# Attention and non-local block in fp32r pairs: score tiles over three bank pairs, the sum row at the batch's head, the second half's residual rows kept whole

## What is computed

```python
q = x1.T @ Wq.T + bq                     # 1024 x 64
k = Wk @ x2 + bk                         # 64 x 1024
v = Wv @ x2 + bv                         # 512 x 1024
xm = v @ softmax(q @ k, axis=1).T + x1   # 512 x 1024
g, theta, phi = convs of x2, xm, x2      # 256 x 1024 each, with their biases
y = (theta.T @ phi / 1024) @ g.T         # no softmax here
out = gamma * (Ww @ y.T + wb - mean) / sqrt(var + 1e-5) + beta + xm
```

## Time and profile before

| | us |
|---|---|
| median of 3 runs | 1065.98 (1063.28 to 1066.46) |
| profiled execution | 1065.61 |
| its span | 1063.8 |
| TensorE busy | 1042.0 (98%) |
| VectorE, ScalarE, GpSimd busy | 722.1, 480.6, 280.5 |

### The profile page before, as it was taken

The page is one execution under the profiler, slowest core; times in us unless marked ns, Lnnn a source line. Parts: engine busy times, 40 slices in busy tenths (PEclk is TensorE's granted clock), DMA queues, the critical chain, the costliest instruction groups (busy, mean ns, idle before and its releaser), DMA issues.

```text
span 1063.8 us, 13869 instructions
## 1 busy us (share of the span) xinstructions
PE 1042.0 (98%) x5104; PEld 850.5 (80%) x5104; DVE 722.1 (68%) x961; ACT 480.6 (45%) x810; POOL 280.5 (26%) x199
## 2 busy tenths in 40 slices
PE   6999999999999999999999999999999999999997
PEld 4688887888778887788877888778887888878886
DVE  6885388844888448884488745886368863788625
ACT  7753355434444345533545325453265532555411
POOL 1412261123501235012360123502244022440220
PEclk9999999999999999999999999999999999999999
DMA  6535251360513605236152351423424344243502
GB/s 237 169 78 143 107 198 43 75 217 27 195 42 73 215 29 197 50 89 198 41 178 58 106 175 64 155 72 106 160 70 149 80 112 146 81 140 78 136 23 79
DMA packets 80627, 122.06 MB, mean 115 GB/s; under 512 B 13104, under 2 KB 46384, under 8 KB 80560
## 3 DMA queue, kind: packets, MB, share of 16 engines
q1 hardware_dynamic: 80560, 121.17, 37.1%
HBM read 70.79 MB, written 16.78 MB: 82 GB/s over the span
## 4 chain that ended last, share of the span: by engine, by line
PE 88%; DVE 6%; DMA 3%; ACT 1%; issue 1%; SPq 0%; DVEq 0%; ACTq 0%
PE pG L573 33%; PE pG L472 13%; PE pG L584 8%; PE pG L480 6%; PE pG L513 4%; PE pG L487 4%; PE pT L594 3%; PE pS L525 3%; PE pT L525 2%; PE pG L594 2%; PE pM L552 2%; PE pM L561 2%; PE pS L451 2%; PE pT L462 2%; DVE xr L902 2%; DMA out_dram<-xr 1%
## 5 line engine op out<-in xcount | busy, mean ns | idle before, releaser
L573 PE MATMUL pG<-pt,vT 128*128 128x512 f32 x1536 | 352.9, 389 | 1.0 <-DVE pt L852 1.0
L573 PEld LDWEIGHTS pG<-pt,vT 128*128 128x128 f32 x1536 | 287.2, 188 | 60.2 <-issue 1.2
L472 PE MATMUL pG<-wv,x2s 128*128 128x512 f32 x768 | 182.9, 393 | 0.5 <-DVE vT L799 0.4
L881 DVE SCALAR_TENSOR_TENSOR xr<-pG,cl,xr 128x512 f32<-128x512 f32 x64 | 48.0, 751 | 189.2 <-PE pG L573 179.9
L931 POOL TENSOR_TENSOR xms<-xr,xms 128x512 fp32r<-128x512 f32 x64 | 87.7, 1370 | 319.6 <-ACT xms L726 319.6
L472 PEld LDWEIGHTS pG<-wv,x2s 128*128 128x128 f32 x768 | 142.1, 188 | 33.3 <-issue 3.3
L726 ACT ACTIVATE xms<-xr 128x512 fp32r<-128x512 f32 x64 | 40.3, 629 | 203.9 <-DVE xr L881 203.9
L852 DVE TENSOR_TENSOR pt<-mv,pt 128x512 fp32r<-128x512 f32 x128 | 89.8, 753 | 35.6 <-ACT pt L703 35.6
L923 POOL TENSOR_TENSOR x2Ts<-x2T_f,x2Ts 128x512 fp32r<-128x512 f32 x64 | 90.5, 1452 | 72.8 <-ACT x2Ts L672 72.7
L927 POOL TENSOR_TENSOR ys<-yf,ys 128x256 fp32r<-128x256 f32 x32 | 27.3, 854 | 306.1 <-ACT ys L694 306.1
L584 PE MATMUL pG<-xms,wth 128*128 128x512 f32 x384 | 90.1, 391 | 0.0
(11 more groups left out here) (112 smaller groups left out, 1420.9 us busy)
## 6 DMA issues: line engine op xcount, KB each, us to landing
mv<-tp SPq DMA_DIRECT2D x512, 64.0 KB, 2.0
...
```

Of the source, the lines that this page charges most:

```text
L472: last = mm(bank, x2s[:, l, c, 128 * m:128 * m + 128], wv[:, r, c, :], start=(c == 0 and n == 0), stop=(c == 3 and n == 2))
L573: last = mm(bank, vT[:, l, m, 128 * c:128 * c + 128], pt(h)[:, r, m, :], start=(m == 0 and n == 0), stop=(m == 7 and n == 2))
```

## The change

It has these parts:

1. Score tiles rotate over three bank pairs: pS, pT, pM. S:t waits for the exp of t-3 from t = 3 on. As pM has other uses, S:2 waits for the copy of gt, S:5 for the low part of GT:1, GT:0 for the exp of tile 2, and M for the exp of tile 5. The lists now have S:0 S:1 S:2, then S:3 S:4, then S:5 S:6 S:7 in batches 1 to 7, where they had S:0 S:1, S:2, S:3, S:4, S:5, S:6 S:7 with other work between.
2. gs stands after v:0 instead of before k, gt before S:0. Its row is kept in a buffer of its own (`grow_b`), which shares memory with the first half's output, so its copy waits for a store.
3. For the second half xr[c] is no longer given up after its split. A new ScalarE step xc:c adds the constant to it in place, wy:1,c multiplies by the gain and adds xr[c], and that is the output: there is no out:1,c. The first half is evicted into the place of the LO part of its own xms (`oh`), with semaphores s_so of its own for the stores; wy:1,c no longer waits for a store. k and q of the next batch wait for these stores. x2T:m waits for theta's last product instead of out:1,m//2.
4. All lists are reordered. In LATER ScalarE has x2T:0 ahead of k, and xs:3 after x1:3; VectorE makes the low part of the next batch's x2:3 between wy:1,1 and wy:1,2 (it was before wy:0,0), and s after k. In FIRST ScalarE has w:0 (rounding of wk) after x2:0, x2:1 and xs:0, and v:4 stands before S:0.

```diff
@@ FIRST (batch 0)
-        "k:0 k:1 v:0 v:1 q:0 q:1 v:2 v:3 S:0 S:1 v:4 S:2 L:0 L:1 L:2 S:3 L:3 gs S:4 G:0 G:1 gt G:2 G:3 v:5 S:5 "
-        "v:6 GT:0 S:6 GT:1 v:7 Y:0 S:7 Y:1 Y:2 Y:3 PV:0,0,0 M:0 PV:0,0,1 M:1 PV:0,1,0 PV:0,1,1 B:0 PV:0,2,0 B:1 "
+        "k:0 k:1 v:0 v:1 q:0 q:1 v:2 v:3 v:4 S:0 S:1 gs gt L:0 L:1 S:2 S:3 L:2 L:3 G:0 G:1 GT:0 S:4 G:2 G:3 v:5 "
+        "GT:1 v:6 S:5 v:7 Y:0 S:6 S:7 Y:1 Y:2 Y:3 PV:0,0,0 PV:0,0,1 PV:0,1,0 M:0 M:1 PV:0,1,1 PV:0,2,0 B:0 B:1 "
...
@@ LATER (batches 1 to 7), pe
-        "gs k:0 k:1 q:0 q:1 v:0 v:1 v:2 S:0 S:1 gt L:0 L:1 S:2 L:2 S:3 L:3 G:0 S:4 G:1 GT:0 G:2 G:3 v:3 S:5 v:4 "
-        "v:5 v:6 GT:1 v:7 Y:0 S:6 S:7 Y:1 Y:2 Y:3 PV:0,0,0 M:0 M:1 PV:0,0,1 PV:0,1,0 PV:0,1,1 B:0 B:1 PV:0,2,0 "
+        "k:0 k:1 q:0 q:1 v:0 gs v:1 v:2 gt S:0 S:1 S:2 L:0 L:1 L:2 L:3 S:3 S:4 G:0 G:1 GT:0 G:2 G:3 v:3 GT:1 v:4 "
+        "v:5 v:6 v:7 S:5 S:6 S:7 Y:0 Y:1 Y:2 Y:3 PV:0,0,0 PV:0,0,1 M:0 M:1 PV:0,1,0 PV:0,1,1 B:0 B:1 PV:0,2,0 "
...
@@ LATER, act
-        "xs:2 xs:3 s x1:2 x1:3 k x2T:0 x2T:1 x2T:2 q x2T:3 x2T:4 x2T:5 v:0 x2T:6 q2 v:1 k2 x2T:7 gs v:2 gt S:0 "
+        "xs:1 xs:2 x1:1 x2:3 x1:2 x1:3 xs:3 s x2T:0 k x2T:1 x2T:2 q x2T:3 x2T:4 v:0 gs q2 k2 x2T:5 v:1 gt x2T:6 "
+        "v:2 x2T:7 S:0 L:0 L:1 L:2 S:1 L:3 S:2 G:0 S:3 G:1 G:2 v:3 T:0 GT:0 v:4 T:1 v:5 GT:1 S:4 G:3 v:6 v:7 T:2 "
...
@@ LATER, dve
+        "k s q v:0 q2 k2 v:1 S:0 v:2 n:0 S:1 tr:0 S:2 n:1 tr:1 G:0 S:3 G:1 n:2 G:2 tr:2 G:3 S:4 n:3 v:3 tr:3 T:0 "
...
+        "th:0,0 B:1 th:0,1 +x2:0 th:1,0 +x2:1 +x2:2 th:1,1 wy:0,0 wy:0,1 out:0 out:1 wy:0,2 wy:0,3 out:2 out:3 "
+        "wy:1,0 wy:1,1 +x2:3 wy:1,2 wy:1,3"
...
+        oh = [at(f"oh{c}", [128, 512], F, rd + 4096 * c + 2048) for c in range(4)]
+        grow_b = at("grow_b", [128, 256], F, rd + 6144)
...
         def s_bank(t):
-            return pT if t % 2 else pS
+            return (pS, pT, pM)[t % 3]
...
             def do_GT(b, r):
                 if r == 0:
-                    wait(eng, "s_colc", b)
+                    wait(eng, "exp", b, 2)
...
             def do_S(b, t):
-                elif t >= 2:
-                    wait(eng, "exp", b, t - 2)
+                elif t == 2:
+                    wait(eng, "s_colc", b)
+                elif t >= 3:
+                    wait(eng, "exp", b, t - 3)
+                    if t == 5:
+                        wait(eng, "GTlo", b, 1)
...
             def do_M(b, k):
+                wait(eng, "exp", b, 5)
...
             def do_x2T(b, m):
                 if b:
-                    wait(eng, "oa", b - 1, 4 + m // 2)
+                    wait(eng, "g", b - 1, G_TH + 3)
...
+            def do_xc(b, c):
+                wait(eng, "xlo", b, 4 + c)
+                done(act(xr[c][:, :], xr[c][:, :], ACT.Identity, bias=cst(c)), "xc")
...
             def do_wy(b, h, c):
-                if h == 0:
-                    wait(eng, "xlo", b, 4 + c)
+                if h:
+                    wait(eng, "xc", b, c)
+                    done(stt(out=xr[c][:, :], in0=bank_of(i), scalar=gain(c), in1=xr[c][:, :],
+                             op0=ALU.mult, op1=ALU.add), "gf")
                 else:
-                    eng.wait_ge(s_st[c], 16 * (2 * b + 1))
-                done(stt(out=xr[c][:, :], in0=bank_of(i), scalar=gain(c), in1=xms(h)[:, c, LO, :].bitcast(F),
-                         op0=ALU.mult, op1=ALU.add), "gf")
+                    done(stt(out=oh[c][:, :], in0=bank_of(i), scalar=gain(c), in1=xms0[:, c, LO, :].bitcast(F),
+                             op0=ALU.mult, op1=ALU.add), "gf")
```

More of the change, by code:

```diff
@@ L236, in xattn_kernel @@
         s_st = [sem(f"s_st{i}") for i in range(4)]
+        s_so = [sem(f"s_so{i}") for i in range(4)]
         s_mv = [sem(f"s_mv{i}") for i in range(8)]
@@ L299, in pt_half @@
                     for t in range(2)]
-        grow = gram_f[2][0:2, 0:256]
+        grow = grow_b[0:2, :]
         def gram_turned(r):
@@ L421, in _ @@
                     for c in range(4):
-                        wait(eng, "oa", b, 4 * h + c)
-                        eng.dma_start(out[b, 128 * c:128 * c + 128, 512 * h:512 * h + 512], xr[c][:, :])\
-                           .then_inc(s_st[c], 16)
+                        dst = out[b, 128 * c:128 * c + 128, 512 * h:512 * h + 512]
+                        if h:
+                            wait_free(eng, b, G_WY + 4 + c)
+                            eng.dma_start(dst, xr[c][:, :]).then_inc(s_st[c], 16)
+                        else:
+                            wait(eng, "oa", b, c)
+                            eng.dma_start(dst, oh[c][:, :]).then_inc(s_so[c], 16)
             for c in range(4):
-                eng.wait_ge(s_st[c], 32 * NB)
+                eng.wait_ge(s_so[c], 16 * NB)
+                eng.wait_ge(s_st[c], 16 * NB)
         @block.tensor
@@ L628, in do_k @@
                 if b:
-                    wait(eng, "oa", b - 1, 3)
+                    for c in (0, 1):
+                        eng.wait_ge(s_so[c], 16 * b)
                 done(act(k1[0:64, :], pS[64:128, :, :], ACT.Copy), "t1k")
@@ L634, in do_q @@
                 if b:
-                    wait(eng, "oa", b - 1, 3)
+                    for c in (2, 3):
+                        eng.wait_ge(s_so[c], 16 * b)
                 done(act(q1[0:64, :], pT[64:128, :, :], ACT.Copy), "t1q")
@@ L706, in do_gs @@
             def do_gs(b):
-                wait(eng, "qlo", b)
                 wait(eng, "s_row", b)
+                if b:
+                    eng.wait_ge(s_so[1], 16 * b)
                 done(act(grow, pM[0:2, 1, 256:512], ACT.Copy), "s_rowc")
@@ L722, in do_B @@
                 done(act(bm[:, HI, k, :], pM[:, k, :], ACT.Copy), "Bhi")
+            def do_xc(b, c):
+                wait(eng, "xlo", b, 4 + c)
+                if b == 0:
+                    eng.wait_ge(s_cst, 4)
+                done(act(xr[c][:, :], xr[c][:, :], ACT.Identity, bias=cst(c)), "xc")
             def do_PV(b, h, c):
@@ L735, in _ @@
             do = dict(w=do_w, x2=do_x2, xs=do_xs, x1=do_x1, k=do_k, q=do_q, k2=do_k2, q2=do_q2, v=do_v, S=do_S, L=do_L, G=do_G,
-                      GT=do_GT, Y=do_Y, x2T=do_x2T, s=do_s, T=do_T, gs=do_gs, gt=do_gt, mts=do_mts, B=do_B, PV=do_PV,
+                      GT=do_GT, Y=do_Y, x2T=do_x2T, s=do_s, T=do_T, gs=do_gs, gt=do_gt, mts=do_mts, B=do_B, xc=do_xc, PV=do_PV,
                       th=do_th)
@@ L892, in do_wy, with do_out @@
                 wait(eng, "g", b, i)
-                if h == 0:
-                    wait(eng, "xlo", b, 4 + c)
-                else:
-                    eng.wait_ge(s_st[c], 16 * (2 * b + 1))
-                done(stt(out=xr[c][:, :], in0=bank_of(i), scalar=gain(c), in1=xms(h)[:, c, LO, :].bitcast(F),
-                         op0=ALU.mult, op1=ALU.add), "gf")
-            def do_out(b, h, c):
-                wait_free(eng, b, G_WY + 4 * h + c)
-                done(stt(out=xr[c][:, :], in0=xr[c][:, :], scalar=cst(c), in1=xms(h)[:, c, HI, :].bitcast(F),
+                if h:
+                    wait(eng, "xc", b, c)
+                    done(stt(out=xr[c][:, :], in0=bank_of(i), scalar=gain(c), in1=xr[c][:, :],
+                             op0=ALU.mult, op1=ALU.add), "gf")
+                else:
+                    done(stt(out=oh[c][:, :], in0=bank_of(i), scalar=gain(c), in1=xms0[:, c, LO, :].bitcast(F),
+                             op0=ALU.mult, op1=ALU.add), "gf")
+            def do_out(b, c):
+                wait_free(eng, b, G_WY + c)
+                done(stt(out=oh[c][:, :], in0=oh[c][:, :], scalar=cst(c), in1=xms0[:, c, HI, :].bitcast(F),
                          op0=ALU.add, op1=ALU.add), "oa")
```

8 lines of the change are left out of this document (4 added, 4 removed), and 38 rows, old and new, of tables (act, dve, pe).

## The result

The changed kernel takes 1079.76 us (median, 1075.69 to 1080.29), the kernel before 1065.94 in the same comparison: ratio 1.0126 [1.0097, 1.0156]. It is slower by 13.8 us, where the forecast was 6.9 faster. The span of its profiled execution is 1077.7 us, 13.9 more than before, so the profile carries the whole loss.

A forecast was written before the change was run, and what follows sets the result against it. TensorE, busy 98% of the span, was taken to bound the kernel. Switches -8.9, old heads -6.5, end -2.0, batch 0 +0.6 and new heads +9.9 gave -6.9 us, from 1065.61 to 1058.7; range 1050 to 1067.

The forecast's parts named there:

- Switching: Score tiles: grouping them saves 0.42 us per joined tile, 9.7 us, less 0.8 for lone sum-row transposes: -8.9 us.
- The end: End of the run: the last wy eviction is itself the output and ends near 1059.3: -2.0 us.
- The heads: Heads of later batches: 6.5 us of old losses in batches 2 to 4 go, new head waits add 9.9 us.
- +9.9 for the new heads: Heads of batches 1 to 7: q's copy late, 1.2 us each (8.4), plus 0.5 in each of three early batches (1.5).
- The upper bound: Later heads: at most 2.7 us lost each, x2T load issued at 24.9 and landing in 6.2 us; total 1067.7.
- The second rival: Later heads: GpSimd holds VectorE's x2:3 for one whole 2.4 us instruction, delaying k and q; slower, 1073.3 at 3.5 us; chance 0.15.
- The middle: Score tiles to PV: new waits of S:2, S:5, M and GT:0 ride behind long work, costed at nothing.
- th: Theta stage at the batch heads: the forecast gave it no gain or loss, taking 11.1 us as its length.
- Batch 0: First batch: later k and v +1.7, v:4 ahead of S:0 -1.7, transposes waiting for the sum row's copy +0.6; net +0.6 us.
- The first rival: Later heads run free, x2T:0 landing in time, so the 9.9 us fall away: 1048.8 us; chance 0.30.

The follow-up runs named there:

- rot_alone: Kernel before with only the three-pair rotation and the middle's new order; heads, output and ends kept as before: 1079.52 us, ratio 1.0140.
- pool_memset: Changed kernel with GpSimd filling x1's low part with zeros instead of subtracting, in batches 1 to 7: 1059.31 us, ratio 0.9953.
- before_memset: Kernel before with GpSimd's subtraction for x1's low part replaced by a zero fill in every batch but the first: 1060.85 us, ratio 0.9958.
- xr_first: Changed kernel with SP's four loads of x1's first half put ahead of the third group of 16 block moves: 1075.51 us, ratio 1.0104.
- all_fix: Changed kernel with x2:3, xs:3, k early, two x2T quarters before stores, xr loads earlier, PV:0,1 and tr:7 earlier on VectorE, batch 0 mended: 1092.34 us.
- wk_first: Changed kernel with w:0, the rounding of wk, first on ScalarE and VectorE in batch 0: 1080.31 us, ratio 1.0126.
- best3: best2 with th's first evictions moved ahead of the x2 splits, and on ScalarE ahead of xc:3: 1049.15 us, ratio 0.9849.
- best2: Changed kernel with the head laid out as before, k ahead of x2T:0, middle and batch 0 mended, x2T loads re-placed on SP: 1059.39 us, ratio 0.9931.
- x2_early: Changed kernel with x2:3's low part moved back ahead of wy and xs:3 right after xs:2: 1073.71 us, ratio 1.0069.

## Why the prediction was wrong, point by point

**Switching, -8.9: right.** From S:0 to the first PV the seven batches take 8.2 us less. Take out gt, which came in ahead of S:0 (its 1.5 us left this stretch), the 1.5 us by which batch 2 was slow before, and Y's new waits, which put PV 2.7 us later in five of them: -8.0, or 1.14 us a batch for the 1.15 forecast (seven times 0.1 for the transposes is 0.7, where I put 0.8). The gain is real, also in rot_alone.

**The end, -2.0: right** (-2.1).

**The heads, forecast +3.4 net (-6.5 and +9.9), measured +11.2.** That is the k and q rows of the table (20.7) less gs (6.5) and gt (1.5) that moved in, and less the 1.5 us of batch 2. Free stages would be 3.63 + 13.07; by that the new heads lose 18.9 us, 2.7 each, for the 1.4 that I put on them. Two steps failed, both in the term "+9.9 for the new heads". I let x2:3 be done "between 21.8 and 23.7" and used it only to time the x2T load; but TensorE begins k at 22.0 and needs that very part in its last matmuls. It was ready 25.3 us after th began in batch 3 (418.9 less 393.57), 1.6 beyond my bound, and 24.9 in four others, so k itself lost 2 us in five of seven batches. The rest of the chain was late with it: in batch 5 the load was issued 26.1 us after th began, was there at 30.4, and q's copy came at 33.6, for the forecast 24.2, 29.0 and 31.6. And I counted half an instruction of GpSimd in the way, where two output additions alone took 3.0 us more than free. Second, I checked S:0 and v:2 against q's copy but not gs, which sits between v:0 and v:1: it waited up to 2.3 us, and the clock fell behind it in batch 1. The upper bound was mis-added as well: 24.9, 6.2 and 2.6 make 33.7, which is 3.1 past 30.6 and not 2.7, so the slow end was 1070.5, not 1067.7; the measured time lies beyond either. The second rival, that ScalarE's and VectorE's head is held for whole GpSimd instructions, is the mechanism (pool_memset, before_memset), at its price of 2.4 us or more a head; I gave it 0.15. The port rule of the Trainium skill (SBUF — State Buffer, Who interferes with whom) said the same, and the runs agree: an addition of 745 ns free, up to 2952 ns here.

**The middle, costed at nothing: wrong by 10.8 us**, 8.1 in PV and 2.7 by the waits for Y. I had asked who waits for the banks, found long covers, and stopped there. But the tiles that come last are also the ones whose exp, normalising, transposes, 16 moves and splits must be done before PV:1,0, and nothing in my working followed them there. SP's list is the same in both kernels, and so I did not look at it: its xr loads now wait behind the moves of the late tile 5 (xr_first: 4.2 us). The rest of PV's loss is VectorE's order, with T:4 and T:5 ahead of PV:0,1's eviction and mt ahead of tr:7 (all_fix: PV at 49.3). The forecast's own last sentence names a stall "before S:3, GT:0 or PV:0"; it came inside PV.

**th, costed at nothing: -1.5.** It had hidden stalls of 0.25 us in a batch, which no row of waits showed; only the stage's length did (11.1 for 10.88).

**Batch 0, +0.6: measured +4.3.** The 3.5 by which the batch grew (2.5 in batch 1's start, and the 0.9 of gs that left it) come with the 0.8 of switching gained inside it. k's end cost 0.7, less than I had. The sum row waited for its weights (1.5) and the transposes for the row (0.6, as forecast), and wy:0,3 waited 1.7 us for an eviction that stood behind two output additions, which I hadn't looked for. Behind the sum row's wait the granted clock fell to 0.50 for a while: the stretch from S:0 to the first PV takes 41.4 us in batch 0 here and 40.1 in wk_first, where the clock stayed full, so some 1.3 us are the clock's. Waits of the kernel before that are gone give the balance.

Sum: -8.0 - 2.1 + 11.2 + 10.8 - 1.5 + 3.5 = 13.9, as measured. The first rival's 1048.8, all heads free, is nearly what best3 takes, by another order and with the middle mended.

Left open: how much of rot_alone's loss in PV is B's place; why best2's batch 3 waited 3.3 us for a move to land, which made TensorE stand 1.96 us (3.7 with the clock that followed), where its other batches and best3 didn't, though batch 3 of x2_early and of all_fix stood in the same place for 1.76 and 1.86; why the x2T load lands later in batches 1 and 3 of the changed kernel; and which of xc:3 and x2:1 held th in best2. That the orders and not the rotation itself cost PV its time is shown by best3, which keeps the rotation and has PV at 49.3; which of the late tile's steps is the longest was not measured.
